# A masked cross attention that keeps keys, queries and results packed on 256 rows and places them by transfers within SBUF

## The chip, the cores and the metric

The kernel runs on one core of one Trainium2 chip. The metric is the device time of one launch in microseconds (us). The program is a decoder of 14 stages that follow one another; the change is in one of them, `L2Cross`, the ninth. PE is TensorE, DVE is VectorE, ACT is ScalarE, POOL is GpSimd, and SP is the queue from which the transfers are issued.

## The reference, cut to what matters

`x` holds 16 batch elements of 112 tokens by 256 features, `ctx` 16 elements of 375 tokens by 256. The stage adds a cross attention of 16 heads of 16 dimensions to `x`, with a mask over the 375 context tokens and with layer norms of queries, keys and values behind their projections:

```python
query = _layernorm(q @ Wq + bq, qn_scale, qn_bias)      # q = _layernorm(x)
key   = _layernorm(kv @ Wk + bk, kn_scale, kn_bias)     # kv = ctx
value = _layernorm(kv @ Wv + bv, vn_scale, vn_bias)
# reshaped to 16 heads of 16
scores = jnp.einsum('bhqd,bhkd->bhqk', query, key) / jnp.sqrt(D_K)
scores = jnp.where(m == 0, NEG_INF, scores)
probs = jax.nn.softmax(scores, axis=-1)
out = jnp.einsum('bhqk,bhkd->bhqd', probs, value)
return out.transpose(0, 2, 1, 3).reshape(bs, -1, D_MODEL) @ Wo + bo
```

## The kernel before

One batch element `n` is worked on in four steps (`NQ = 4`), each with four heads (`HQ = 4`), so that the stage has 64 steps `i = 4n + r`. The text calls the steps by `r`: **quarter 0, 1, 2 and 3** of PE's loop. Each engine runs an order that is written out by hand and waits on semaphores; nothing is reordered.

Each head sits on 32 rows of the 128: one row that carries the softmax shift (or, in the results, the denominator), 16 rows of data and 15 rows of zeros (`Z = 32`). So 256 features take 512 rows (`W = 512`), in four blocks of 128.

One pass of PE's loop, from `scores(i + 1)` to `lowest_turned(i + 1)`:
- `scores(i+1)` (four matmuls, one a head), then `scores_turned(i)` (12 matmuls, the scores once more with the context tokens on the rows), which needs `shifted(i)` from DVE;
- then, each released by one of the four minima that DVE takes from `scores(i+1)` (`lowest`, line 3330, "max" 0 to 3, since the matmuls write the PSUM banks that it has read): two pieces of other work (a and b), then `attend(i-1)` (12 matmuls), and, after the fourth minimum, `lowest_turned(i+1)`, which turns the row minima.

DVE in the same pass takes the four minima, some other work, `shifted(i+1)` as soon as `lowest_turned(i+1)` is there, and then more work that stands in its queue ahead of the next minima. ACT takes `exps(i)`, some other work and `results(i-1)`; POOL zeroes the masked probabilities (`only_kept(i)`, two halves), which `attend(i)` waits for.

The other work by quarter, before: 0: the turn of `x` for n+2 and the spread of the reciprocals of n-2; 1: keys and values of n+2, two of three parts (`keys_values`), the queries of n+1 turned, and the denominators of n-1 gathered by matmuls; 2: the keys of n+1 turned in four blocks (12 transposes), and the output projection of n-2 over four blocks; 3: the third part of keys and values, and the query projection of n+2. The bias of keys and values is added by POOL (`biased`) to a copy that ACT takes out of PSUM. SP loads `ctxT` and the two masks; the weights of the next stage are fetched from the start (`prefetch`).

`L3Cross`, a later stage of the same program with 64 steps of the same kind but without a mask and without norms, already has the packed layout with transfers within SBUF; its rows are in the trace of before.

## Time and profile before

| | |
|---|---|
| median of 3 runs | 3768.4 us (3765.77 to 3771.09) |
| profiled execution | 3750.74 us, its span 3748.9 us |
| PE / PEld / DVE / ACT / POOL busy | 85% / 58% / 49% / 32% / 24% of the span |
| the changed stage | from 2014.4 to 2444.3 us of the span |
| `L3Cross` | from 3239 to 3587.7 us |

The page gives busy time over the whole program; the changed stage is about a ninth of it, so that the stage has to be read alone. In the timeline views each row has a start, the time until the last merged instruction ended, the engine, the line, and after the shapes the count; in brackets stands the idle time before it and what ended it. The difference of two starts is what a group takes in its queue.

### The profile page before, as it was taken

All of it is one profiled execution on the core that took longest, in us unless ns stands there. A gap on an engine that the chain in (4) does not pass through costs nothing. (4 is left out here: it accounts for less than half of the span.)

```text
span 3748.9 us, 76885 instructions
## 1 busy us (share of the span) xinstructions
PE 3184.8 (85%) x30862; PEld 2176.7 (58%) x30862; DVE 1819.2 (49%) x4553; ACT 1188.1 (32%) x2326; POOL 913.9 (24%) x751
## 2 busy tenths in 40 slices
PE   7886999999996875879857899879997788999988
PEld 2333445544566773555624555569996675566655
DVE  7886443344124342442267666643334582355543
ACT  1222222222213322131232655522221452244432
POOL 1000432233000000230624877712111220104000
PEclk9887999999997986998978999979998888999989
DMA  4212000000116011341731111058886210021100
GB/s 147 68 56 75 21 9 8 16 8 0 49 31 43 4 23 30 82 129 45 228 87 33 32 29 28 10 213 331 329 326 234 95 55 15 28 73 54 43 8 15
DMA packets 183358, 291.65 MB, mean 78 GB/s; under 512 B 85585, under 2 KB 153639, under 8 KB 173716
## 3 DMA queue, kind: packets, MB, share of 16 engines
q1 hardware_dynamic: 175572, 266.95, 23.3%
q0 software_dynamic: 7488, 20.46, 1.7%
q8 instruction: 220, 3.60, 0.4%
q14 instruction: 78, 0.64, 0.1%
HBM read 243.33 MB, written 28.48 MB: 73 GB/s over the span
## 5 line engine op out<-in xcount | busy, mean ns | idle before, releaser
L2581 PE MATMUL ps<-L_ffn_xsT,arena 128*128 128x128 f32 x2584 | 305.9, 277 | 0.8 <-DVE L_ffn_xsT L2397 0.7
L2581 PEld LDWEIGHTS ps<-L_ffn_xsT,arena 128*128 128x128 f32 x2584 | 298.5, 194 | 2.9 <-DVE L_ffn_xsT L2397 2.7
L161 POOL TENSOR_TENSOR rstd<-nsc,mhalf 112x4 f32<-112x4 f32 (+1 forms) x24 | 40.1, 1669 | 954.6 <-DVE nsc L154 953.6
L793 POOL TENSOR_TENSOR L_xattn_rn<-L_xattn_ss,mhalf 125x16 f32<-125x16 f32 (+1 forms) x64 | 185.7, 2901 | 324.4 <-DVE L_xattn_ss L847 324.4
L3242 POOL TENSOR_TENSOR L_xattn_pT<-L_xattn_pT,L_xattn_keep 125x678 int32<-125x678 int32 x128 | 190.4, 1509 | 71.9 <-ACT L_xattn_pT L3497 71.9
L686 PE MATMUL ps<-L_attn_prod,arena 128*32 128x448 f32 (+31 forms) x672 | 157.2, 537 | 44.5 <-DVE L_attn_prod L508 44.5
L2489 ACT ACTIVATE L_ffn_silu<-ps,arena 128x128 f32<-128x128 f32 x280 | 102.9, 368 | 269.3 <-PE ps L2581 252.5
L2406 DVE SCALAR_TENSOR_TENSOR L_ffn_hT<-ps,arena,L_ffn_silu 128x128 f32<-128x128 f32 x280 | 97.9, 350 | 156.8 <-ACT L_ffn_silu L2489 156.8
L961 PE MATMUL ps<-arena,L_xattn_cT 128*125 128x512 f32 x384 | 170.3, 596 | 4.3 <-DVE L_xattn_unit L840 4.3
L508 DVE TENSOR_TENSOR L_attn_prod<-arena,L_attn_k 128x448 f32<-128x448 f32 (+10 forms) x336 | 160.4, 545 | 2.3 <-PE ps L686 2.3
L976 PE MATMUL ps<-L_xattn_unit,L_xattn_cn 125*128 125x512 f32 x336 | 159.2, 634 | 0.0
L2594 PE MATMUL ps<-arena,L_ffn_hT 128*128 128x256 f32 x646 | 154.7, 384 | 4.8 <-ACT L_ffn_ys L2498 4.3
L2278 POOL DMA_INDIRECT L_ffn_rows_out<-L_ffn_ys,L_ffn_dest x78 | 80.0, 1025 | 320.0 <-DVE L_ffn_ys L2415 304.2
L845 DVE TENSOR_REDUCE L_xattn_ss<-L_xattn_sq 125x16 f32<-125x1024 f32 (+1 forms) x64 | 78.1, 1220 | 126.3 <-ACT L_xattn_sq L888 126.3
L3929 DVE TENSOR_REDUCE L_xattn_low<-ps 112x1 f32<-112x375 f32 (+1 forms) x192 | 117.8, 667 | 29.0 <-PE ps L4124 29.0
L961 PEld LDWEIGHTS ps<-arena,L_xattn_cT 128*125 128x125 f32 x384 | 69.5, 187 | 104.0 <-issue 77.3
L2594 PEld LDWEIGHTS ps<-arena,L_ffn_hT 128*128 128x128 f32 x646 | 117.4, 191 | 20.8 <-ACT L_ffn_ys L2498 8.0
L3330 DVE CUSTOM_DVE_ANT_0 y<-ps,y 112x375 f32<-112x375 f32 x256 | 124.3, 540 | 6.9 <-PE ps L3603 6.8
L4045 ACT ACTIVATE L_xattn_pT<-ps 125x672 f32<-125x672 f32 x128 | 86.5, 728 | 112.8 <-PE ps L4134 112.8
L2273 POOL DMA_INDIRECT L_ffn_xs<-L_ffn_rows_in,L_ffn_source x78 | 77.5, 993 | 178.9 <-DVE L_ffn_dest L2384 86.2
L1696 PE MATMUL ps<-arena,L_mlp_hT 128*112 128x256 f32 x512 | 117.9, 383 | 0.0
L888 ACT ACTIVATE L_xattn_sq<-ps 125x1024 f32<-125x1024 f32 (+1 forms) x64 | 65.6, 1024 | 163.7 <-PE ps L961 163.7
(574 smaller groups left out, 6713.2 us busy)
## 6 DMA issues: line engine op xcount, KB each, us to landing
arena<-in_L_ffn_up SPq DMA_DIRECT2D x35, 2056.0 KB, 7.7
arena<-in_L_ffn_down SPq DMA_DIRECT2D x35, 1152.0 KB, 8.8
L_xattn_ctxT<-in_ctxT SPq DMA_DIRECT2D x48, 375.0 KB, 3.8
arena<-in_L_ffn_up SPq DMA_DIRECT2D x43, 384.0 KB, 4.5
L_attn_a<-L_attn_skew SPq DMA_DIRECT2D x16, 784.0 KB, 5.8
L_xattn_ctx<-in_ctx SPq DMA_DIRECT2D x30, 375.0 KB
arena<-L_xattn_kp SPq DMA_DIRECT2D x64, 93.8 KB, 3.3
L_xattn_mask<-in_mask SPq DMA_DIRECT2D x32, 164.1 KB, 8.5
```

Source lines behind the costliest of these rows:

```text
L508: nc.vector.tensor_tensor(prod[:, i % RING, :, t0:T], by_batch(q[:, b])[:, :, t0:T], k[:, b, :, PAD + t0 - j:PAD + T - j], ALU.mult).then_ ...
L686: nc.tensor.matmul(by_batch(ps[32 * cg:32 * cg + 32, g % 2, 0:N4])[:, :, t0:T], self.scale[:, w:w + 32], prod[:, i % RING, :, t0:T], start ...
L793: nc.gpsimd.tensor_tensor(rn[0:r, i], ss[0:r, i], core.mhalf[0:r, 0:H], ALU.pow).then_inc(po_r.step("root", i), 1)
L961: ins = nc.tensor.matmul(ps[0:height(i), bank(i) + b, :], lhs, w[:, k, cols], start=(k == 0), stop=(k == KD - 1))
L976: ins = nc.tensor.matmul(ps[:, 4 + 2 * m + b, :], cn[:, t, m * 128:(m + 1) * 128], unit[:, W + t, b * 512:(b + 1) * 512], start=(s == 0), ...
L1696: nc.tensor.matmul(ps[0:T, 4 + u, 0:D], hT[:, i, u * T:(u + 1) * T], self.w2[:, i, :], start=(i == 0), stop=False)
L2489: ins = nc.scalar.activation(silu[:, b % 2], src, ACT.Silu, bias=self.bias(i % WU, m))
L2581: ins = nc.tensor.matmul(ps[:, 2 + b % 4, half * TS:(half + 1) * TS], self.up(i % WU, k, half * HM + m), xsT[:, i % 2, k], start=(k == 0), ...
L2594: ins = nc.tensor.matmul(ps[:, 6 + i % 2, 0:D], hT[:, i % HR, m], self.down(i % WD, m), start=(m == 0), stop=(m == HM - 1))
L3242: nc.gpsimd.tensor_tensor(p, p, keep[:, n % 2].unsqueeze(1).to_broadcast([SP_, 2, ST * TP]), ALU.mult).then_inc(po_e.step("kept", half), 1)
L3330: nc.vector.tensor_tensor_reduce(masked[:, h], ps[0:T, 4 * g + h, 0:S], drop[:, n % 2], -1.0, 3e38, ALU.add, ALU.min, low[:, i % 2, h * Z: ...
L3929: nc.vector.tensor_reduce(heads(low[:, i % 2])[:, h:h + w, 0:1], ps[0:T, b:b + w, 0:S], AX.X, ALU.max, negate=True).then_inc(ve_m.step("ma ...
```

## The change

Queries, keys and results stay packed on 256 rows, in two blocks of 128 (`KD = 2`), with the columns mixed so that the heads of one group of rows lie together. Where the score matmuls need 32 rows a head, SP places the rows by transfers from SBUF to SBUF: four for the keys (`kp` to `kT`), four for the queries (`qk` to `q`), and on the way back one for the denominators (`o` to `den`) and four for the results (`o` to `op`), per batch element.

With it: the keys are turned in two blocks (6 transposes) in quarter 0, the queries in two, the projection has two matmuls; the denominators are 16 rows by 112 that a transfer brings, their reciprocal is taken on 16 rows and spread by two matmuls with `of_head`. DVE adds the bias of keys and values straight from PSUM (`keys_values`), which takes the three copies from ACT and the three additions from POOL. POOL adds the output bias to `x` (`shifted`), once a batch element. The statistics of keys and queries, which DVE took in five pieces over the four quarters, are taken behind `shifted` of quarters 1 and 2, and ACT normalises queries and keys two batch elements ahead, in quarter 3. The turn of `x` moves to quarter 3 and three elements ahead.

```diff
-        self.k = a.take(SP_, ST, self.W)
+        self.k = a.take(SP_, ST, D)
 ...
+            def keys(n):
+                sp.wait_ge(ac_kT.sem, ac_kT.at(n, "kT0"))
+                sp.wait_ge(ve_kT.sem, ve_kT.at(n, "kT1"))
...
+                for h in range(HQ):
+                    sp.dma_start(in_heads(kT[:, n % 2], h), of_rows(kp, h, S)).then_inc(k_in[n % 2], DMA)
...
+            def results(n):
+                sp.wait_ge(ac_p.sem, ac_p.at(NQ * n + NQ - 1, "o"))
...
+                sp.dma_start(den[:, n % 2], o[0:128:Z, n % 2].rearrange("p (j t) -> p j t", j=NQ)).then_inc(o_in[n % 2], DMA)
+                for h in range(HQ):
+                    sp.dma_start(of_rows(op[:, n % 2], h, T), in_heads(o[:, n % 2], h)).then_inc(o_in[n % 2], DMA)
...
+            for n in range(NB):
+                if n + 1 < NB:
+                    keys(n + 1)
+                    queries(n + 1)
+                if n >= 1:
+                    results(n - 1)
+                if n == 1:
+                    run.prefetch(sp)
...
         @block.gpsimd
-            def biased(n, s):
-                nc.gpsimd.tensor_tensor(r, r, self.bkv, ALU.add).then_inc(po_b.step("bias", s), 1)
...
+            nc.gpsimd.memset(q[:, :, :], 0.0).then_inc(zeroed, 1)
+            rows_of(0).then_inc(zeroed, 1)
             nc.gpsimd.memset(low[:, :, :], 0.0).then_inc(zeroed, 1)
+            rows_of(1).then_inc(zeroed, 1)
...
+                if r == 3 and n + 2 < NB:
+                    root_q(n + 2)
+                    root_k(n + 2)
                 only_kept(i)
...
         @block.vector
+            def keys_values(n, s, bank):
+                dve.wait_ge(pe_k.sem, pe_k.at(n, "kv", s))
+                nc.vector.tensor_tensor(raw[:, slot(n, s)], ps[0:SP_, bank, :], self.bkv, ALU.add).then_inc(ve_kv.step("kv", s), 1)
...
+                if r == 0 and n + 1 < NB:
+                    queries(n + 1, 4 * g)
+                    kept(n + 1)
+                if r == 1 and n + 2 < NB:
+                    key_statistics(n + 2, 0)
+                    key_statistics(n + 2, 1)
+                if r == 2:
+                    if n + 2 < NB:
+                        query_variance(n + 2)
+                        key_statistics(n + 2, 2)
+                        for s in range(ST):
+                            key_variances(n + 2, s)
                     if n >= 1:
-                        inverses(n - 1, 4 * g + 3, T)
+                        inverses(n - 1)
+                if r == 3:
+                    if n >= 1:
+                        divided(n - 1, 4 * g + 1)
...
         @block.scalar
+                if r == 3 and n + 2 < NB:
+                    query_normed(n + 2)
+                    keys_normed(n + 2)
...
         @block.tensor
+                if r == 0 and n + 1 < NB:
+                    keys_turned(n + 1, 0, a)
+                    ten.wait_ge(ve_m.sem, ve_m.at(i + 1, "max", 1))
+                    keys_turned(n + 1, 1, b)
...
-                if r == 1 and n >= 1:
-                        denominators(n - 1, 4 * g + 3, T)
```

DVE, from the end of quarter 2 of a batch element in the middle of the stage to the first minimum of quarter 3 (`qm` is written by `shifted`, `st_k` and `st_q` are the statistics of keys and queries, the ISA row on `low` is a minimum). Before:

```order
L3361 TENSOR_TENSOR x<-x,ps 112x256
L3343 TENSOR_TENSOR L_xattn_qm<-L_xattn_q,ps 128x112
L204 BN_STATS stats<-x 112x6
L3307 BN_STATS L_xattn_st_k<-L_xattn_raw 125x6 x2
L3330 ISA y,L_xattn_low<-ps,y 112x375
```

and now:

```order
L3433 TENSOR_TENSOR x<-x,ps 112x256
L3415 TENSOR_TENSOR L_xattn_qm<-L_xattn_q,ps 128x112
L3347 BN_STATS L_xattn_st_q<-y 112x6
L3351 BN_AGGR L_xattn_mv_q<-L_xattn_st_q 112x2
L3353 TENSOR_SCALAR L_xattn_eps_q<-L_xattn_mv_q 112x1
L3378 BN_STATS L_xattn_st_k<-L_xattn_raw 125x6 x2
L3385 BN_AGGR L_xattn_mv_k<-L_xattn_st_k 125x2 x6
L3388 TENSOR_SCALAR L_xattn_eps_k<-L_xattn_mv_k 125x6
L3421 RECIPROCAL L_xattn_inverse<-L_xattn_den 16x112
L3402 ISA y,L_xattn_low<-ps,y 112x375
```

Between `shifted` and the first minimum stood three instructions; now there are thirteen.

ACT, from the end of quarter 3 into quarter 0 (`pT` is written by `exps`, `xT` by the turn of `x`, `y` here holds the queries, the `arena` rows from `raw` are keys or values being normalised). Before:

```order
L3486 COPY L_xattn_raw<-ps 125x512
L3505 COPY L_xattn_least<-ps 128x1
L3507 ACTIVATE L_xattn_o<-ps,L_xattn_least 128x112
L3474 ACTIVATE arena<-L_xattn_raw,L_xattn_off_k,L_xattn_rs_k 125x16x16 x3
L3497 ACTIVATE L_xattn_pT<-ps 125x6x112 x2
```

and now:

```order
L3554 COPY L_xattn_xT<-ps 128x224
L3575 COPY L_xattn_least<-ps 128x1
L3577 ACTIVATE L_xattn_o<-ps,L_xattn_least 128x112
L3530 ACTIVATE y<-y,L_xattn_off_q,L_xattn_rs_q 112x256
L3537 ACTIVATE arena<-L_xattn_raw,L_xattn_off_k,L_xattn_rs_k 125x256 x3
L3567 ACTIVATE L_xattn_pT<-ps 125x6x112 x2
L3560 ACTIVATE L_xattn_kp<-ps,arena 128x375
```

The three normalisations in front of `exps` were those of the values; now they are those of the keys that PE turns in this same quarter 0, with the queries' ahead of them and the packed keys' way out of PSUM (`kp`) behind.

PE, quarter 2. Before:

```order
L3603 MATMUL ps<-arena,L_xattn_q 112x375 x4
L3613 MATMUL ps<-L_xattn_qm,arena 125x112 x12
L3590 MATMUL ps<-ident,arena 128x125 x6
L3627 MATMUL ps<-L_xattn_pT,arena 32x113 x12
L3590 MATMUL ps<-ident,arena 128x125 x6
L3646 MATMUL ps<-arena,L_xattn_on 112x256 x4
L3618 MATMUL ps<-ident,L_xattn_low 128x112
```

and now:

```order
L3648 MATMUL ps<-arena,L_xattn_q 112x375 x4
L3658 MATMUL ps<-L_xattn_qm,arena 125x112 x12
L3630 MATMUL ps<-arena,L_xattn_ctxT 125x512 x2
L3619 MATMUL ps<-arena,L_xattn_xT 112x256 x2
L3672 MATMUL ps<-L_xattn_pT,arena 32x113 x12
L3685 MATMUL ps<-arena,L_xattn_on 112x256 x2
L3663 MATMUL ps<-ident,L_xattn_low 128x112
```

The transposes of the keys have gone to quarter 0, the third part of keys and values and the query projection have come from quarter 3, and the projection (`on`) follows `attend` directly.

## Rows read from the trace of the kernel before

**Rows 1.** Windows: length, busy PE, PEld, DVE, ACT, POOL, PE's clock, DMA share, GB/s

```profile
2086.67:2389.82 303.15, 278.61 (x3384) 173.16 (x3384) 197.53 (x764) 179.27 (x372) 237.70 (x217) 0.98 0.10 28
2389.82:2435.20 45.38, 34.90 (x573) 23.79 (x572) 29.29 (x115) 24.13 (x51) 32.22 (x27) 1.00 0.01 2
2435.20:2444.28 9.08, 5.99 (x52) 4.56 (x52) 2.44 (x7) 1.13 (x3) 0.96 (x1) 1.00 0.00 0
```

**Rows 2.** Timeline of PE, one batch element, quarters 2, 3, 0, 1

```profile
2332.70 0.90 PE L3603 MATMUL ps<-arena,L_xattn_q 32*112 32x375 f32 x8
2335.32 0.86 PE L3590 MATMUL ps<-ident,arena 125*128 125x125 f32 x6
...
2339.86 0.90 PE L3603 MATMUL ps<-arena,L_xattn_q 32*112 32x375 f32 x8
...
2342.02 1.98 PE L3584 MATMUL ps<-arena,L_xattn_ctxT 128*125 128x512 f32 x4 [0.48 <-DVE L_xattn_low L3330]
2343.84 1.03 PE L3571 MATMUL ps<-arena,L_xattn_xT 128*112 128x256 f32 x4
2344.79 0.79 PE L3627 MATMUL ps<-L_xattn_pT,arena 125*32 125x113 f32 x24
...
2345.76 0.90 PE L3603 MATMUL ps<-arena,L_xattn_q 32*112 32x375 f32 x8
...
2348.33 0.60 PE L3640 MATMUL ps<-ident,y 112*128 112x112 f32 x4
...
2349.83 0.90 PE L3603 MATMUL ps<-arena,L_xattn_q 32*112 32x375 f32 x8
...
2356.30 0.60 PE L3577 MATMUL ps<-ident,y 112*128 112x112 f32 x4
...
2357.68 0.90 PE L3603 MATMUL ps<-arena,L_xattn_q 32*112 32x375 f32 x8
```

**Rows 3.** Timeline of DVE in the same batch element

```profile
2340.77 0.73 DVE L3307 BATCH_NORM_STATS2 L_xattn_st_k<-L_xattn_raw 125x6 f32<-125x256 f32 x2
2341.43 0.53 DVE L3330 CUSTOM_DVE_ANT_0 y<-ps,y 112x375 f32<-112x375 f32 x1
...
2346.51 0.43 DVE L3291 BATCH_NORM_STATS2 L_xattn_st_q<-y 112x6 f32<-112x256 f32 x1
...
2347.26 0.54 DVE L3330 CUSTOM_DVE_ANT_0 y<-ps,y 112x375 f32<-112x375 f32 x1
```

**Rows 4.** Timeline of DVE near the stage's start, variances of keys

```profile
2030.89 0.48 DVE L3314 BATCH_NORM_AGGREGATE L_xattn_mv_k<-L_xattn_st_k 125x2 f32<-125x6 f32 x6
...
2050.06 1.43 DVE L3317 TENSOR_SCALAR L_xattn_eps_k<-L_xattn_mv_k 125x6 f32<-125x6 f32 x1
```

**Rows 5.** Timeline of ACT, quarter 3 into 0

```profile
2345.65 0.16 ACT L3505 COPY L_xattn_least<-ps 128x1 f32<-128x1 f32 x1 [0.97 <-PE ps L3627]
...
2346.10 1.59 ACT L3474 ACTIVATE arena<-L_xattn_raw,L_xattn_off_k,L_xattn_rs_k 125x256 f32<-125x256 f32 x3
2347.58 1.33 ACT L3497 ACTIVATE L_xattn_pT<-ps 125x672 f32<-125x672 f32 x2
```

**Rows 6.** Groups by line and shape over the stage's loop

```profile
L3490 ACT ACTIVATE arena<-ps,arena 128x375 f32<-128x375 f32 x30 | 20.0, 667 | 3.2 <-PE ps L3590 3.0
```

**Rows 7.** The later stage `L3Cross`: DVE, SP and PE timelines

```profile
3475.00 0.83 DVE L3940 RECIPROCAL L_xattn_inverse<-L_xattn_den 16x112 f32<-16x112 f32 x1
...
3249.11 2.52 SPq L3837 DMA_DIRECT2D arena<-L_xattn_kp  x4
...
3255.76 0.90 PE L4124 MATMUL ps<-arena,L_xattn_q 32*112 32x375 f32 x8 [1.57 <-DMA L_xattn_q<-L_xattn_qp]
```

**Rows 8.** PE at the stage's start and in its last steps

```profile
2041.18 0.90 PE L3603 MATMUL ps<-arena,L_xattn_q 32*112 32x375 f32 x8
...
2427.64 1.98 PE L3646 MATMUL ps<-arena,L_xattn_on 128*112 128x256 f32 x8 [0.65 <-ACT L_xattn_o L3507]
```

**Rows 9.** Window in one quarter 2 with a lower clock, columns as in rows 1

```profile
2182.00:2184.00 2.00, 2.00 (x21) 1.48 (x21) 1.17 (x5) 1.58 (x3) 0.85 (x1) 0.50 0.00 0
```

More of the change, by code:

```diff
@@ L3190, in _, with context @@
         def _(sp):
-            for n in range(NB):
-                if n == 2:
-                    run.prefetch(sp)
+            def context(n):
                 if n >= 2:
@@ new lines, in queries @@
+            def queries(n):
+                sp.wait_ge(ve_qT.sem, ve_qT.at(n, "q"))
+                if n >= 2:
+                    sp.wait_ge(ve_s.sem, ve_s.at(NQ * (n - 2) + NQ - 1, "shifted"))
+                for h in range(HQ):
+                    sp.dma_start(in_heads(q[:, n % 2], h), of_rows(qk[:, n % 2], h, T)).then_inc(q_in[n % 2], DMA)
+            def results(n):
+                sp.wait_ge(ac_p.sem, ac_p.at(NQ * n + NQ - 1, "o"))
+                if n >= 2:
+                    sp.wait_ge(ve_d.sem, ve_d.at(n - 2, "divided"))
+                sp.dma_start(den[:, n % 2], o[0:128:Z, n % 2].rearrange("p (j t) -> p j t", j=NQ)).then_inc(o_in[n % 2], DMA)
+                for h in range(HQ):
+                    sp.dma_start(of_rows(op[:, n % 2], h, T), in_heads(o[:, n % 2], h)).then_inc(o_in[n % 2], DMA)
@@ new lines, in _ @@
+            for n in range(2):
+                context(n)
+                masks(n)
+            keys(0)
+            queries(0)
+            context(2)
+            for n in range(NB):
[6 more added lines that the diff above has]
+                    run.prefetch(sp)
+                if n + 3 < NB:
+                    context(n + 3)
+                if n + 2 < NB:
+                    masks(n + 2)
@@ L3374, in _ @@
             query_statistics(0, 2)
[L3375 to L3378 removed]
             for s in range(ST):
+                keys_values(0, s, 3 + s)
                 key_statistics(0, s)
@@ L3422, in _ @@
+                if r == 1 and n + 2 < NB:
+                    key_statistics(n + 2, 0)
+                    key_statistics(n + 2, 1)
+                if r == 2:
+                    if n + 2 < NB:
+                        query_variance(n + 2)
+                        key_statistics(n + 2, 2)
+                        for s in range(ST):
+                            key_variances(n + 2, s)
                     if n >= 1:
-                        inverses(n - 1, 4 * g + 3, T)
-                    if n + 1 < NB:
-                        queries(n + 1, 4 * g)
@@ L3517, in _ @@
             act.wait_ge(run.arrived, run.loads)
-            for s in range(ST):
-                keys_values(0, s, 3 + s)
             query_normed(0)
-            keys_values(1, 0, 3)
-            keys_values(1, 1, 4)
+            turned(2, 0)
             keys_normed(0)
-            keys_turned(0, 1, 2)
-            keys_turned(0, 3, 5)
+            keys_turned(0, 1)
+            query_normed(1)
             values_normed(0)
-            keys_values(1, 2, 3)
+            keys_normed(1)
             for i in range(STEPS):
@@ L3575, in queries_turned @@
                 ten.wait_ge(ac_qn.sem, ac_qn.at(n, "qn"))
-                for j in range(NQ):
-                    ins = nc.tensor.transpose(ps[:, bank, j * T:(j + 1) * T], qn[:, j * 128:(j + 1) * 128], core.ident[0:T, 0:T])
-                ins.then_inc(pe_q.step("qT"), 1)
+                transposes(core, ps[:, bank], qn, T, KD).then_inc(pe_q.step("qT"), 1)
             def keys_values(n, s, bank):
@@ L3644, in project @@
                 ten.wait_ge(ve_d.sem, ve_d.at(n, "divided"))
-                for j in range(NQ):
-                    ins = nc.tensor.matmul(ps[0:T, bank, 0:D], on[:, n % 2, j * T:(j + 1) * T], self.wo[:, j, :], start=(j == 0), stop=(j == NQ - 1))
+                for m in range(KD):
+                    ins = nc.tensor.matmul(ps[0:T, bank, 0:D], on[:, n % 2, m * T:(m + 1) * T], self.wo[:, m, :], start=(m == 0), stop=(m == KD - 1))
                 ins.then_inc(pe_o.step("out"), 1)
@@ L3723, in _ @@
                     queries(n + 2, b)
-                if i + 1 == STEPS:
-                    spread(n - 1, b)
+                if r == 3:
+                    if n + 3 < NB:
+                        turn(n + 3, a)
+                    if n >= 1:
+                        if i + 1 < STEPS:
+                            ten.wait_ge(ve_m.sem, ve_m.at(i + 1, "max", 1))
+                        spread(n - 1, b)
                 if i >= 1:
@@ L3749, in _ @@
             project(NB - 2, 4)
-            denominators(NB - 1, 1, 0)
             spread(NB - 1, 2)
```

360 lines of the change are left out of this document (153 added, 207 removed).

## The prediction

> **What bounds the kernel now.** The page first: the changed stage is 430 us of 3749, and the other 13 stages keep their instructions, so everything below is about that stage. Next the windows: in the middle of the stage PE is busy 278.6 of 303.2 us, POOL 237.7, DVE 197.5, ACT 179.3 [rows 1]. That looks like a PE bound, but the reader is to see in PE's timeline where it waits: one batch element takes 24.98 us from 2332.70 to 2357.68, in quarters of 7.16 (quarter 2), 5.90 (3), 4.07 (0) and 7.85 (1) [rows 2]. In each quarter PE stands still only where the other queues hold it: in quarter 3 the keys and values start 0.48 late, on the first minimum of DVE [rows 2]. PE goes on 0.59 after DVE starts its first minimum (2341.43 to 2342.02) [rows 2, 3]. So what counts is not DVE's busy share but how much work stands in its queue between `shifted` and the next minima; there is little slack, and whoever puts work there pays. The same holds for ACT between its `results` and `exps`.
>
> **The change, quarter by quarter.** I lay the new queues out with the in-queue times of before (start to next start) and count from the start of `scores`.
>
> PE's own work falls. Two blocks of keys instead of four save 6 transposes, 0.86. Two projection matmuls of four save half of 1.8, so 0.9. The denominators and half of the turned queries go: 2356.30 to the next `scores` at 2357.68 is 1.38, of which `lowest_turned` (0.2) and two transposes (0.22) stay, so about 0.95 [rows 2]. Together 2.7 us a batch element. If PE alone counted, 14 elements would give 38 us. I do not expect to see it, for these reasons:
>
> Quarter 2. PE now has `keys_values` and the query projection here, as in the old quarter 3, and DVE has two pairs of statistics ahead of its minima (0.66 each [rows 3]) instead of the update of `x`, its statistics and one pair; its first minimum starts at about 1.6, as in the old quarter 3. So `attend` starts at 5.0 (before: 2339.86 to 2344.79 = 4.93) [rows 2]. The projection waits for `results` of the `attend` just ahead of it, which the second half of the key transposes used to cover; uncovered it is 0.79 of `attend` and 0.65 of idle time, as in the last steps [rows 8]. Then 0.9 for two projection matmuls and 0.2: 5.0 + 1.44 + 0.9 + 0.2 = 7.55, against 7.16.
>
> Quarter 3. Behind `shifted` (ended 0.57 into the quarter: the pair at 2340.77 was at 0.91, with 0.34 of statistics of `x` ahead of it that have moved away, an estimate by the query's similar 0.43) stand now: variance of the queries 0.75, a pair of statistics 0.66 [rows 3], six aggregations 0.48 [rows 4] and the epsilon 0.1 (an estimate by one of these six), the reciprocal on 16 rows 0.8 (0.83 busy in the later stage [rows 7]; the one before, of 112 rows by 16, stood elsewhere). Sum 3.35: DVE's first minimum starts there, not at 1.57. PE goes on at 3.95; its second piece waits for the second minimum, 1.07 behind the first's start (2347.26 to 2348.33 [rows 2, 3]): 4.4, the spread of four short matmul passes 0.6, `attend` and `lowest_turned` 0.97 (2344.79 to 2345.76 [rows 2]): 6.0, against 5.90. PE has only 3.8 of work there, so 2.2 us of PE's gain is idle time.
>
> Quarter 0. ACT: `attend` of quarter 3 starts at 5.0; `results` starts 0.86 later and the next in the queue another 0.45 later (2344.79, 2345.65, 2346.10 [rows 2, 5]), so at 6.35. Then the queries' normalisation 0.5 and the keys' three 1.48 (2346.10 to 2347.58, the same shapes for the values [rows 5]): 8.3, which is 2.3 into quarter 0. PE wants to turn these very keys at 1.7 and starts at 2.45; 0.8 for both blocks and 0.75 for `attend`: 4.0. The turned queries reuse the bank of the first block, so they wait for ACT: `exps` 2.3 to 3.55, then the packed keys, 0.67 [rows 6]: 4.25. With 0.22 and 0.25: 4.75, against 4.07.
>
> Quarter 1. Nothing new ahead; the denominators and half of the turned queries fall away: 7.85 - 0.95 = 6.9, and with `divided` on 224 instead of 448 columns and now in quarter 0, about 6.7. The bias additions on DVE (not in the trace in this shape; between the 0.42 of the query's 256 columns and, by columns, 0.8) lie behind the minima, beside 3.6 us of PE's matmuls for keys and values, and are hidden: uncovered they would cost 0.7 in quarter 1.
>
> Sum 7.55 + 6.0 + 4.75 + 6.7 = 25.0 against 24.98: nothing, for the twelve elements in the middle.
>
> Transfers. In the later stage, four transfers of keys and four of queries took from 3249.11 to 3255.76, 6.65 us, until the scores started [rows 7]. Here the packed keys are ready at 4.3 of quarter 0 and the scores want them at the start of quarter 3, 16 us later; SP has 13 issues of 0.63 (2.52 for four [rows 7]) and three loads, some 10 us of 25. The next stage's weights are now issued in the second element, behind `results`, 5 us of SP; still hidden. Results have two quarters. What hides all this is the loop; at both ends there is no loop.
>
> The ends. Start: POOL writes 2.1 us more (`q`, twice `kT`, less `k` and `qn`), the keys and values of element 1 (5.5) now come before the first key transposes, and 6.65 of transfers stand before the first scores; against it, the weights' scaling leaves the path. From the last of element 0's work I get the first scores at 45 instead of 41.18 [rows 8], +4 (3 to 5). Tail: 9.08 [rows 1] from the last `attend` on; the gathering matmuls, the widening on ACT and the wide projection (-2.5) give way to five transfers, 5 * 0.63 + 1.6 of landing (6.65 - 8 * 0.63) = 4.8: +2.3 (1 to 3).
> The first two elements have no projection or no reciprocals: there quarter 1 gives its 1.2 twice and quarter 3 0.6: -3. In the last two there are no statistics, keys or values, PE's saving is real: 45.38 [rows 1] shrinks by 1.3 + 2.0 (a quarter 1 without denominators, a quarter 2 without transposes and half the projection) and 0.8 + 0.9, less 1: -4.
>
> Total: 0 + 4 + 2.3 - 3 - 4 = -0.7 us. Against the profiled execution: 3750.7 - 0.7 = 3750.0. The runs' median is 17.7 above that execution, so 3768.4 - 0.7 = 3767.7; I say 3768.
>
> **Rules of the skill that speak against it.** A small DVE operation can be held up by POOL: the epsilon of the keys took 1.43 us once, while six small ones take 0.48 [rows 4]. In quarter 3 the two epsilons now stand in the chain that PE waits for; by my layout POOL has nothing to do just then. The Trainium skill, "SBUF — State Buffer", section "SBUF: two separate sides", says that POOL and a DVE operation in a two-port mode hold a shared pair of ports exclusively, and the other blocks for the whole instruction. The trace agrees where both met; by that rule the forecast stands only while POOL is idle there, otherwise the rival below holds.
>
> **The rivals.**
> 1. PE's saving comes through. That needs the minima to start early in quarter 3 and the keys to be normalised in time. For it: quarter 3's 3.35 is a sum of seven in-queue times, and waits of PE can shift into one another. Half of the lost 2.7, over 12 elements, is 16 us: 3752; all of it 3736. Against: ACT's order is fixed. Chance 0.22 for anything faster than 0.2%.
> 2. The clock. PE now stands still for 2.2 us in quarter 3 and for 0.8 in quarter 0. In a quarter 2 of before PE's clock fell to half (0.50 at 2182 to 2184 [rows 9]), behind short matmuls; three such drops in the middle explain 303.15 against 12 times 24.98 = 299.8, so 1.1 each [rows 1, 2]. Place: quarter 3; one drop in each element, less the three: + 9 * 1.1 = 10 us, 3778. It decides from seven more drops on (7.5 us). Against: in the stretch from 2389.82, where PE was busy for 34.9 of 45.4 us, the clock was 1.00 [rows 1]. Chance 0.17. The Trainium skill, "TensorE: Matmul & The Clock Gate", section "HAM oscillation — how this bites in real kernels", says that waits between bursts throw the array back to its lower clock; by it this would be the likelier way.
> 3. DVE's chain is longer than laid out: an epsilon held by POOL for up to 1.3 (1.43 less 0.1 [rows 4]) in quarter 3, once or twice an element, + 12 * 1.3 = 16 us: 3784. It needs POOL to be late from quarter 2. Chance 0.11.
> 4. The forecast, within 0.2%: 0.50.
>
> **The numbers.** A change of 0.2%, 7.5 us, is about what a measurement of this kernel can tell from none. Quarters that I may have wrong by 0.3 us, over 12 elements, make 4 us; the two ends 2 more. Own range 3761 to 3776. For 8 in 10 it reaches to half of rival 1 and to rivals 2 and 3: 3755 to 3784. Faster 0.22, same 0.50, slower 0.28.
>
> **What would show it.** In the profile after: PE's timeline with quarters of 7.5, 6.0, 4.8 and 6.7; a wait of about 2 us before the turn of `x` or the spread, ended by DVE's minimum; the key transposes waiting for ACT's normalised keys and the turned queries for `kp`; the projection waiting for `o`; no wait of `scores` for a transfer but at the start; first scores 4 us later. The forecast is wrong if quarter 3 is near 4.5 (DVE's queue was not the bound), if the clock is 0.50 in many windows, or if `scores` waits for transfers in the loop.

## The result, and the profile after

The changed kernel is slower: 3790.53 us median (3782.62 to 3795.19, 6 runs) against 3769.32 us (3765.77 to 3773.78) for the kernel before, run beside it. The ratio is 1.0052, 95% interval 1.004 to 1.0065. The prediction said 3768 us, range 3755 to 3784, "same" the likeliest. It was wrong, and the time lies outside the range.

The changed stage takes 448.7 us in place of 428.5, 20.2 more, about the whole of the difference of 21.2 between the medians. (The two profiled executions are further apart, 3793.1 and 3748.9 us; the other 24 us lie outside the stage, where the instructions are the same, and in the changed kernel run again they are 4. So the stage is read from the profiles and the whole from the medians.) Cut at the first `scores`, at the quarter 3 of element 1, at the quarter 3 of element 13, and at the last `scores`:

| part of the stage, us | before | after | difference | forecast |
|---|---|---|---|---|
| start, until the first `scores` | 26.7 | 32.0 | +5.3 | +4 |
| first two elements | 45.5 | 44.0 | -1.5 | -3 |
| twelve elements in the middle | 303.2 | 314.4 | +11.3 | 0 |
| last steps, until the last `scores` | 33.8 | 35.0 | +1.2 | -4 |
| tail | 19.3 | 23.3 | +4.0 | +2.3 |

The forecast cut the last two parts at the last `attend` and not at the last `scores`. By its own cut they are 45.4 and 47.2 us (+1.8, forecast -4), and 7.7 and 11.1 us until TensorE is done (+3.4, forecast +2.3).

The windows of the changed kernel, columns as in [rows 1]: the middle, the last steps (here they reach into the last one), and the tail.

```profile
2106.95:2421.39 314.44, 267.39 (x3145) 164.94 (x3145) 211.80 (x766) 145.64 (x314) 201.40 (x192) 0.89 0.19 54
2421.39:2460.37 38.98, 28.09 (x476) 19.45 (x476) 24.50 (x96) 18.70 (x40) 27.74 (x24) 0.87 0.08 21
2460.37:2480.10 19.73, 12.36 (x93) 8.29 (x93) 7.34 (x17) 2.38 (x6) 5.58 (x5) 0.50 0.03 7
```

The seventh value is TensorE's granted clock. In the middle it is 0.89 where it was 0.98 [rows 1]. At the end it is 0.87 and 0.50, where it was 1.00 throughout. That is the first thing to see, and most of the document follows from it.

TensorE's timeline for one element, quarters 2, 3, 0 and 1, the counterpart of [rows 2] (L3648 is `scores`):

```profile
2308.65 0.90 PE L3648 MATMUL ps<-arena,L_xattn_q 32*112 32x375 f32 x8
...
2310.85 1.98 PE L3630 MATMUL ps<-arena,L_xattn_ctxT 128*125 128x512 f32 x4 [0.66 <-DVE L_xattn_low L3402]
...
2313.62 0.79 PE L3672 MATMUL ps<-L_xattn_pT,arena 125*32 125x113 f32 x24
2315.08 1.12 PE L3685 MATMUL ps<-arena,L_xattn_on 128*112 128x256 f32 x4 [0.66 <-ACT L_xattn_o L3577]
...
2316.22 0.90 PE L3648 MATMUL ps<-arena,L_xattn_q 32*112 32x375 f32 x8
2316.98 0.92 PE L3658 MATMUL ps<-L_xattn_qm,arena 32*125 32x112 f32 x24
2320.07 0.41 PE L210 MATMUL ps<-ident,L_xattn_xn 112*128 112x112 f32 x2 [2.16 <-DVE L_xattn_low L3402]
2320.53 1.14 PE L3679 MATMUL ps<-L_xattn_inverse,arena 16*128 16x112 f32 x4
2321.60 1.36 PE L3672 MATMUL ps<-L_xattn_pT,arena 125*32 125x113 f32 x24
...
2323.27 1.61 PE L3648 MATMUL ps<-arena,L_xattn_q 32*112 32x375 f32 x8
2324.66 1.46 PE L3658 MATMUL ps<-L_xattn_qm,arena 32*125 32x112 f32 x24
2326.05 1.51 PE L3636 MATMUL ps<-ident,arena 125*128 125x125 f32 x6
2327.49 0.79 PE L3672 MATMUL ps<-L_xattn_pT,arena 125*32 125x113 f32 x24
...
2328.65 0.90 PE L3648 MATMUL ps<-arena,L_xattn_q 32*112 32x375 f32 x8
```

The reader is to see three things. The waits are where the prediction put them: 0.66 for the projection's `o`, 2.16 for the first minimum of quarter 3. Behind that wait the same instructions take longer: L3672 takes 0.79 us in quarter 2 and 1.36 in quarter 3, the scores 0.90 and then 1.61, the turned scores 0.92 and 1.46. And at 2327.49, in quarter 0, they are back at 0.79. Quarters 2 and 1 take 7.57 and 6.50 us (forecast 7.55 and 6.7); quarters 3 and 0 take 7.05 and 5.38 (forecast 6.0 and 4.75).

VectorE in quarter 3, the counterpart of [rows 3]:

```profile
2316.23 0.42 DVE L3433 TENSOR_TENSOR x<-x,ps 112x256 f32<-112x256 f32 x1 [2.08 <-PE ps L3685]
2316.57 0.26 DVE L3415 TENSOR_TENSOR L_xattn_qm<-L_xattn_q,ps 128x112 f32<-128x112 f32 x1
2316.75 0.42 DVE L3347 BATCH_NORM_STATS2 L_xattn_st_q<-y 112x6 f32<-112x256 f32 x1
...
2317.42 0.15 DVE L3353 TENSOR_SCALAR L_xattn_eps_q<-L_xattn_mv_q 112x1 f32<-112x1 f32 x1
2317.49 0.74 DVE L3378 BATCH_NORM_STATS2 L_xattn_st_k<-L_xattn_raw 125x6 f32<-125x256 f32 x2
2318.15 0.49 DVE L3385 BATCH_NORM_AGGREGATE L_xattn_mv_k<-L_xattn_st_k 125x2 f32<-125x6 f32 x6
2318.68 0.17 DVE L3388 TENSOR_SCALAR L_xattn_eps_k<-L_xattn_mv_k 125x6 f32<-125x6 f32 x1
2318.76 0.84 DVE L3421 RECIPROCAL L_xattn_inverse<-L_xattn_den 16x112 f32<-16x112 f32 x1
2319.53 0.47 DVE L3402 CUSTOM_DVE_ANT_0 y<-ps,y 112x375 f32<-112x375 f32 x1
```

The first minimum starts 3.31 us into the quarter (2316.22 to 2319.53); the forecast was 3.35. The two epsilons take 0.15 and 0.17, so POOL does not hold them up. The first row also shows what the experiments use: ahead of the update of `x`, VectorE waits 2.08 us for the projection.

The clock, in windows of this stretch (quarter 3, quarter 0, and the stretch in which the instructions are slow):

```profile
2316.22:2323.27 7.05, 4.83 (x64) 3.27 (x63) 5.08 (x23) 1.91 (x5) 5.22 (x8) 0.81 0.00 0
2323.27:2328.65 5.38, 5.38 (x67) 3.97 (x66) 3.53 (x12) 4.45 (x10) 2.06 (x3) 0.61 0.01 3
...
2320.50:2327.00 6.50, 6.47 (x66) 4.97 (x67) 3.78 (x15) 3.64 (x9) 3.15 (x4) 0.51 0.01 3
```

From just after the end of the 2.16 us wait until 2327 the clock is at its lower level, 1.2 in place of 2.4 GHz, while TensorE is busy for all of the stretch. The text calls such a stretch a fall. Over the elements 2 to 12 the fall begins between 0.3 us before and 1.6 us after the end of this wait. In quarter 0 TensorE then has no idle time at all (5.38 of 5.38 us), so the slow matmuls are themselves what the quarter takes. Windows of half a microsecond over the whole middle show 12 such falls in 12 elements, 68.3 us at the lower level in all; before there were 3, with 10.2 us. A fall lasted 3.4 us in four elements and 6.8 us in the other eight. Against the 10.57 us that quarters 3 and 0 take together without a fall (below, e10), a fall of 3.4 us cost 0.8 to 0.9 and one of 6.8 us 1.8 to 2.2 us.

### The profile page after: what moved, and what is told of

The parts are those of the page before. It is cut to its first block and busy times, and to the rows that moved or that the text cites. A ratio compares the mean times of both kernels' runs of the same rounds, so it can differ in the third digit from the quotient of the medians.

```text
span 3793.1 us, 76365 instructions
## 1 busy us (share of the span) xinstructions
PE 3173.7 (84%) x30540; PEld 2169.6 (57%) x30540; DVE 1840.0 (49%) x4555; ACT 1142.3 (30%) x2246; POOL 866.8 (23%) x720
## 5 line engine op out<-in xcount | busy, mean ns | idle before, releaser
L2581 PE MATMUL ps<-L_ffn_xsT,arena 128*128 128x128 f32 x2584 | 313.7, 281 | 32.9 <-DVE L_ffn_xsT L2397 23.6
L686 PE MATMUL ps<-L_attn_prod,arena 128*32 128x448 f32 (+31 forms) x672 | 157.0, 537 | 45.4 <-DVE L_attn_prod L508 45.4
```

The lines of the kernel that those rows point to most:

```text
L686: nc.tensor.matmul(by_batch(ps[32 * cg:32 * cg + 32, g % 2, 0:N4])[:, :, t0:T], self.scale[:, w:w + 32], prod[:, i % RING, :, t0:T], start ...
L2581: ins = nc.tensor.matmul(ps[:, 2 + b % 4, half * TS:(half + 1) * TS], self.up(i % WU, k, half * HM + m), xsT[:, i % 2, k], start=(k == 0), ...
```

## The experiments

The theory (A): with the granted clock at 1.00, the new quarters would add up to the old ones as forecast. The VectorE work behind `shifted` in quarter 2 makes TensorE wait 2.16 us in quarter 3, the clock falls behind that wait, and the slow matmuls of quarters 3 and 0 make the loss. The rival (B): the moved VectorE work and the new waits make the loss by themselves, and the lower clock costs nothing. Each kernel ran beside the kernel before. The absolute times named in the expectations of the first four are on the scale of the first comparison, 3769 for the kernel before; in theirs it had 3754.9, so the differences are what to compare. "Middle" is the time of the twelve elements, with the falls of the clock in them and the time at the lower level, counted in windows of half a microsecond.

| kernel | median, minus before beside it, us | ratio, 95% interval | stage | middle | falls, us low |
|---|---|---|---|---|---|
| before | | | 428.5 | 303.2 | 3, 10.2 |
| changed | +21.2 | 1.0052, 1.004 to 1.0065 | 448.7 | 314.4 | 12, 68.3 |
| e10, changed again | +18.5 | 1.0054, 1.0036 to 1.0073 | 443.9 | 311.5 | 11, 58.0 |
| e1, nine fillings | +8.4 | 1.0029, 1.0014 to 1.0043 | 437.4 | 305.1 | 0 |
| e5, four fillings | -1.6 | 0.9997, 0.9984 to 1.001 | 427.9 | 298.5 | 4, 13.7 |
| e4, reciprocal early | -2.4 | 0.9997, 0.9984 to 1.001 | 420.9 | 290.6 | 4, 13.7 |
| e2, statistics early | -27.0 | 0.9937, 0.992 to 0.9955 | 399.9 | 273.0 | 0 |
| e3, both early | -24.8 | 0.9943, 0.9928 to 0.9959 | 406.1 | 276.9 | 0 |
| e6, statistics spread | -37.2 | 0.9895, 0.9873 to 0.9916 | 396.4 | 267.5 | 1, 6.8 |
| e7, ends too | -40.7 | 0.9894, 0.9875 to 0.9914 | 388.4 | 265.7 | 0 |
| e8, before with an idle | +28.5 | 1.0064, 1.0039 to 1.0089 | 458.4 | 328.6 | 7, 23.9 |
| e9, other wait filled | +76.1 | 1.0194, 1.0175 to 1.0213 | 508.4 | 368.8 | 12, 164 |

(The middle of e1 is twelve times its element of 25.43 us. The low time of e9 is twelve falls of 13.7 us. The profile behind stage and middle is of one execution, the median of five or more, and the two can differ by some us: e4 and e6 do by 5.)

**Filling the wait: e1, e5.** TensorE gets extra matmuls among the scores of quarter 3, in a region that the real scores overwrite:

```diff
                 for h in range(HQ):
+                    if h == 3 and i % NQ == 0 and 2 <= n <= NB - 1:
+                        for w in range(9):    # 4 in e5
+                            nc.tensor.matmul(ps[0:T, 4 * g + h, 0:128], self.wo[:, 0, 0:T], self.wo[:, 1, 0:128], start=True, stop=True)
                     p = slice(h * Z, (h + 1) * Z)
```

> The changed kernel, with nine more TensorE matmuls of 128 columns (some 2 us) put among the scores of each quarter 3, in the stretch in which TensorE waited 2.16 us for the first minimum. They write a region that the real scores then overwrite, so the results are the same; TensorE only has more to do. Theory A (the clock: the 2.16 us idle in quarter 3 makes the granted clock fall to 0.50 for 3.4 or 6.8 us in each element, and that costs about 1 us of an element): the clock stays at 1.00 in the middle elements, quarter 3 takes 6.1 to 6.3 in place of 7.1 and quarter 0 4.7 to 4.9 in place of 5.3, 10 to 14 us less in all, 3776 to 3781. Theory B (the clock only falls where VectorE is waited for anyway; the quarters are longer because the moved VectorE work and the new waits are): 3790 or up to 5 us more, quarter 3 stays at 7.1.

Measured: no fall in the middle, and quarter 0 at 4.67 us as expected. Quarter 3 takes 6.67, not 6.2: nine fillings are more than the wait can hold, TensorE is busy 6.50 of 6.67 us there. About 13 us less than the changed kernel (+8.4 in place of +21.2). More work on the busiest engine made the kernel faster, which B doesn't allow; the size was left for e5.

> The changed kernel with four of the nine filling matmuls (some 0.9 us of TensorE work that leaves the results as they are). The nine kept the clock at 1.00, but made quarter 3 take 6.67 us, because they held up the work behind them; four leave the first minimum as the last to come, as in the changed kernel, and VectorE's chain as it is. Theory A (the clock costs 0.87 us in quarter 3 and 0.64 us in quarter 0): TensorE's idle falls to about 1.2 us, the clock stays at 1.00, quarter 3 takes 6.0 and quarter 0 4.67; 1.5 us per middle element, 16 to 20 us less than the changed kernel, that is 0 to +4 us beside the kernel before. Theory B (the clock is only a sign, the 2.16 us of VectorE work cost it all): within 3 us of the changed kernel, +20 beside the kernel before. If the clock still falls with 1.2 us idle, the same as B in time, with the clock at 0.50 as before.

Measured: 0.9997 of the kernel before, 22.8 us less than the changed kernel by the differences of the medians. The windows of one element, quarters 2, 3, 0 and 1, columns as in [rows 1]:

```profile
2204.30:2211.88 7.58, 6.25 (x70) 3.79 (x69) 4.56 (x15) 4.16 (x10) 3.13 (x3) 1.00 0.41 112
2211.88:2217.79 5.91, 5.41 (x73) 3.83 (x72) 5.08 (x23) 1.70 (x4) 4.08 (x7) 1.00 0.00 0
2217.79:2222.45 4.66, 3.68 (x66) 2.53 (x65) 3.49 (x12) 4.59 (x11) 3.11 (x3) 1.00 0.02 5
2222.45:2228.96 6.51, 6.37 (x66) 3.14 (x66) 4.54 (x14) 1.45 (x4) 6.43 (x6) 1.00 0.28 80
```

With the clock at 1.00 the quarters are 7.58, 5.91, 4.66 and 6.51, in sum 24.66; the forecast was 7.55, 6.0, 4.75 and 6.7, in sum 25.0. TensorE's wait before the turn of `x` is 0.44 us, and not the 1.2 that I had expected of four fillings. VectorE's busy time in quarter 3 is the same 5.08 us as in the changed kernel. Quarter 3 takes as long as a quarter 3 of the changed kernel without a fall (5.91, below), so the fillings changed nothing of the schedule but TensorE's idle time. A holds, B is refuted. Four falls are left in the middle all the same, all of 3.4 us, in quarters 3 and 0.

**The changed kernel again: e10.**

> The changed kernel as it is, once more beside the kernel before, for the size of the difference and to see whether the clock falls as often in another execution. If the drops belong to the schedule: 1.004 to 1.0065 of the kernel before (15 to 24 us more), 12 falls in the 12 middle elements, most of them 6.8 us long. If they were a matter of that one execution: fewer than 8 falls.

Measured: 1.0054, 11 falls. Two elements of this execution are worth more than the sum, since there nothing was edited. Quarters 3 and 0 of one element without a fall, and of one with a long fall:

```profile
2190.55:2196.46 5.91, 3.69 (x65) 2.47 (x64) 5.08 (x23) 1.81 (x4) 4.08 (x7) 1.00 0.00 0
2196.46:2201.12 4.66, 3.68 (x66) 2.53 (x65) 3.49 (x12) 4.59 (x11) 3.11 (x4) 1.00 0.01 4
2240.51:2247.51 7.00, 4.78 (x65) 3.22 (x64) 5.08 (x23) 1.91 (x5) 5.17 (x8) 0.82 0.00 0
2247.51:2252.89 5.38, 5.38 (x66) 3.98 (x66) 3.53 (x12) 4.43 (x10) 2.10 (x3) 0.60 0.01 3
```

The same instructions, the same idle before the first minimum: 10.57 us without the fall, 12.38 with it. A long fall costs 1.8 us.

**The other wait: e9.** The fillings stand in quarter 0 (`i % NQ == 1`, three of them) in place of quarter 3.

> The changed kernel with three filling matmuls (0.4 to 0.6 us of TensorE work that leaves the results as they are) in quarter 0, where TensorE waits 0.84 us for the first minimum; the wait of 2.16 us in quarter 3 stays whole. It asks which idle the clock follows. Theory A1 (the one long wait of quarter 3 brings the clock down): the clock falls in nearly every element as in the changed kernel, and the time is within 4 us of it, or up to 5 us more. Theory A2 (any idle of the element counts alike, so filling a short wait helps as much as filling a part of the long one): the clock stays up in most elements, 10 us or more less than the changed kernel, as the four matmuls in quarter 3 gave 20.

Measured: much slower than either theory said. The clock fell in every element, as A1 has it, from 3.7 to 4.0 us into quarter 3, where the long wait ends; filling in quarter 0 did not help, as A2 wanted it. The time was off by 50 us. Quarter 3 and quarter 0:

```profile
2276.18:2283.38 7.20, 5.04 (x65) 3.41 (x64) 5.08 (x23) 1.91 (x5) 5.37 (x8) 0.76 0.01 2
2283.38:2292.69 9.31, 9.31 (x72) 6.56 (x72) 3.54 (x12) 4.68 (x10) 2.80 (x3) 0.50 0.00 0
```

Quarter 0 takes 9.31 in place of 5.38 us, all of it busy and at the lower clock. The fillings stand ahead of the last scores, on which the minima and everything behind them wait, and take some 1.5 us of it at the lower rate; the other 2.4 come from the rest of the quarter, all of which now runs at 0.50 in place of 0.61. Each fall lasts 13.7 us. 3.9 us in each of 15 elements make 59; the stage is 59.7 us longer than the changed kernel's, and the medians 55 to 58. Three such matmuls here lost over 50 us, where four in quarter 3 gained over 20. Why the clock stayed down for twice as long isn't settled.

**Moving the cause away: e2, e3, e4.** VectorE's own wait of 2.08 us ahead of the update takes the statistics (e2), the reciprocal (e4) or both (e3):

```diff
                 if r == 2:
                     if n + 2 < NB:
                         keys_values(n + 2, 2, 4 * g)
                         queries_biased(n + 2, 4 * g + 1)
+                        query_variance(n + 2)         # e2, e3
+                        key_statistics(n + 2, 2)
+                        for s in range(ST):
+                            key_variances(n + 2, s)
+                    if n >= 1:                        # e3, e4
+                        inverses(n - 1)
                     if n >= 2:
                         update(n - 2, 4 * g + 2)
```

(and they go from behind `shifted`, where they stood.)

> The changed kernel, with the moved statistics of quarter 2 (query_variance, the third key_statistics, the key_variances; 2.0 us of VectorE) put ahead of the update of x and of the shifted queries, into 2.08 us in which VectorE waited for the projection; the reciprocal stays behind. Theory A (the clock and the idle of quarter 3 that brings it down): TensorE's idle in quarter 3 falls from 2.16 to about 0.2, the clock stays up; quarter 3 takes 4.9 to 5.2, quarter 0 4.7 to 4.9, about 2.6 us per element, 14 elements: 36 us less, 3754 (3748 to 3762). Theory B (schedule alone, the clock has no part): 2.0 x 14 = 28 us less, 3762, with quarter 0 still at 5.3. Theory C (the 2 us is needed elsewhere: quarter 3 is bound by ScalarE's or POOL's chain at 6 us as it was before the change): quarter 3 at 5.9 to 6.2, 15 us less, 3775.

> As the run with the statistics ahead of the update, and the reciprocal of the denominators (0.77 us) ahead of it too. VectorE then starts the first minimum of quarter 3 about 1.3 us into the quarter, when the scores have just come. Theory A: no idle before the first minimum beyond the minimum's own 0.5; but 2.8 us of work stand in 2.08 us of waiting, so the update and the shifted queries come 0.7 us later and quarter 2 may grow by that. The sum against the run with the statistics alone: -0.8 in quarter 3 and up to +0.7 in quarter 2, so between 0 and 10 us less: 3744 to 3754. Theory C (quarter 3 held at 6 us by ScalarE or POOL): same as that run within 2 us, or 10 us more if quarter 2 grows.

> The changed kernel, with only the reciprocal (0.77 us of VectorE) put ahead of the update of x in quarter 2. TensorE's idle in quarter 3 becomes 1.4 us in place of 2.16. Theory A: if an idle of 1.4 us still brings the clock down, 0.77 x 14 = 11 us less, 3780; if it doesn't, 11 + 12 = 23 us less, 3768. Theory B (no part of the clock): 11 us less, 3780, whatever the clock shows.

Measured: e2 is 48 us faster than the changed kernel and 27.0 faster than the kernel before (A said 36 less than the changed one, B 28, C 15, so all three were too small). In e2, quarter 3 of an element: VectorE's first minimum, and TensorE's next work.

```profile
2293.78 0.83 DVE L3421 RECIPROCAL L_xattn_inverse<-L_xattn_den 16x112 f32<-16x112 f32 x1
2294.55 0.47 DVE L3402 CUSTOM_DVE_ANT_0 y<-ps,y 112x375 f32<-112x375 f32 x1
```

```profile
2293.25 0.90 PE L3647 MATMUL ps<-arena,L_xattn_q 32*112 32x375 f32 x8
2294.01 0.92 PE L3657 MATMUL ps<-L_xattn_qm,arena 32*125 32x112 f32 x24
2295.08 0.41 PE L210 MATMUL ps<-ident,L_xattn_xn 112*128 112x112 f32 x2
```

The minimum starts 1.30 us into the quarter and TensorE shows no wait. Quarter 3 takes 3.89 us, quarter 0 4.67, the element 22.65. I had expected 4.9 at best for quarter 3, and C 6: neither ScalarE nor POOL was the next bound there. Of the saving of TensorE's work that the first rival of the prediction spoke of, 2.7 us an element, most is there (24.98 - 22.65 = 2.33), and it needed only this.

What is left in quarter 0 is a wait of 0.84 us before the turn of the keys:

```profile
2299.69 0.83 PE L3635 MATMUL ps<-ident,arena 125*128 125x125 f32 x6 [0.84 <-DVE L_xattn_low L3402]
```

```profile
2297.97 1.57 ACT L3536 ACTIVATE arena<-L_xattn_raw,L_xattn_off_k,L_xattn_rs_k 125x256 f32<-125x256 f32 x3
```

The row names VectorE's minimum, but TensorE here also waits for ScalarE's normalised keys, and these are ready at 2299.54, 0.15 us before it goes on. That is the wait for ScalarE that the prediction had in quarter 0 (the expectation of e9 took it for one on the minimum).

e3 is no better: its quarter 3 takes 4.21. The 2.8 us of work do not fit into the wait, the shifted queries come later, and the turned scores wait for them; I had put that delay into quarter 2, and it shows in quarter 3. The row of e3, and the wait for the first minimum that is left in e4:

```profile
2274.94 0.92 PE L3656 MATMUL ps<-L_xattn_qm,arena 32*125 32x112 f32 x24 [0.52 <-DVE L_xattn_qm L3415]
```

```profile
2259.13 0.41 PE L210 MATMUL ps<-ident,L_xattn_xn 112*128 112x112 f32 x2 [1.51 <-DVE L_xattn_low L3402]
```

e4 decides between A's two branches: with this wait of 1.51 us, only 4 falls are left in the middle, most elements have quarter 3 at 5.25 and quarter 0 at 4.67, and the time is 23.6 us less than the changed kernel. 23 was the number of "the clock stays up"; 11 that of the schedule alone. It does not show that the length of the single wait decides: e5, with no wait over 0.84 us in most elements, has four falls too.

**The idle without the change: e8.**

```diff
                     if n + 2 < NB:
                         key_statistics(n + 2, 0)
+                        for w in range(5):
+                            nc.vector.bn_stats(junk[:, 30 * (n % 7) + 6 * w:30 * (n % 7) + 6 * w + 6], self.bkv[:, 0:D])
```

> The kernel before, with five more bn_stats (1.75 us of VectorE, into a tile that nothing reads) ahead of the first minimum of quarter 3, so that TensorE's idle there is 2.2 us in place of 0.48; nothing else of the change is in it. Theory A (an idle of some 2 us in quarter 3 brings the clock down in this loop, whatever the layout): the clock is at 0.50 for 3.4 us or more in nearly each element as in the changed kernel; 1.75 us and 1 to 1.5 us for the clock, 14 elements: 38 to 46 us more than the kernel before. Theory B (the drops come from something else in the new layout, short matmuls or transfers): the clock stays, 1.75 x 14 = 24 us more.

Measured: +28.5 us, between the two theories. TensorE's wait in quarter 3 is 2.12 us, as meant. Two quarters 3, one with a fall and one without:

```profile
2279.29:2288.45 9.16, 7.04 (x67) 3.75 (x66) 5.80 (x20) 2.05 (x4) 3.98 (x3) 0.81 0.08 11
2307.52:2315.06 7.54, 5.42 (x67) 3.12 (x66) 5.80 (x20) 2.05 (x4) 3.98 (x3) 1.00 0.09 26
```

A fall costs 1.4 to 1.7 us here, but there are 7 in the middle, not 12, and each of 3.4 us. Six of them come behind the wait in quarter 3, where the kernel before had none; the seventh is in quarter 2, as its three were. So the old layout, given the same wait, shows falls in quarter 3 in half of the elements, and the new one in nearly all. The wait is a cause and not the only condition; in the new layout a wait for ScalarE's `kp` and less matmul work stand around it (TensorE busy 267.4 of 314.4 us in the middle, against 278.6 of 303.2 [rows 1]). Which of these makes the rest was not tried.

**Further on the same way: e6, e7.** e6 is e2 with `key_statistics(n + 2, 0)` between the two `keys_values` of quarter 1, and with `statistics(n - 2)` ahead of `shifted` in quarter 3. e7 is e6 with the first queries' transfers on ScalarE's queue and a semaphore of their own for the denominators.

```diff
-            queries(0)                                    # SP, at the start
+            for h in range(HQ):                           # ScalarE, ahead of values_normed(0)
+                act.dma_start(q[h * Z + 1:h * Z + 1 + HD, 0].rearrange("p (j s) -> p j s", j=NQ), qk[h % 2 * 64:(h % 2 + 1) * 64, 0, h // 2 * T:(h // 2 + 1) * T]).then_inc(q_in[0], DMA)
...
-                dve.wait_ge(o_in[n % 2], (n // 2 + 1) * (HQ + 1) * DMA)
+                dve.wait_ge(d_in[n % 2], (n // 2 + 1) * DMA)
```

> The kernel with the statistics ahead of the update (23 to 27 us faster than the kernel before), and two more moves of VectorE work into its own waits: key_statistics(n+2, 0) between the two keys_values of quarter 1 (it waits 1.03 us there), and statistics(n-2) of quarter 3 ahead of the shifted queries (it waits 0.82 us there). If the first minimum is what ends TensorE's waits of 0.66 us in quarter 2 and 0.84 us in quarter 0: 0.65 less in one and 0.35 less in the other, 1.0 us per element, 14 us less, 3714 on the scale on which the kernel before has 3755. If ScalarE or POOL is right behind (POOL's masks end 1.3 us before the weights times values in quarter 2, ScalarE's 2 x exp in quarter 0 follow keys_normed at once): only one of the two comes through, 5 to 9 us less.

> As the run with the statistics spread, and two changes of the transfers at the ends: the four transfers of the first queries are issued by ScalarE's queue beside SP's four for the first keys, and the denominators have a semaphore of their own, so that their reciprocal doesn't wait for the four transfers of the results. Start: the first scores waited for the last transfer of queries, whose issue came after the keys'; 2.0 to 2.5 us less. Tail: the last reciprocal and the spread (2.1 us) run beside the transfers of the results, about 2 us less. Together 4 us less (3 to 5) than that run. Rival: a transfer's fixed time and not its turn in the queue sets both; then 0 to 2 us less.

Measured: e6 has quarter 2 at 6.95 (0.63 less) and quarter 0 unchanged at 4.67, so one of its two moves came through, and the middle is 5.5 us shorter than in e2. In quarter 0 the first minimum then waits for the scores themselves and starts no earlier, 0.97 us into the quarter; and TensorE's wait of 0.84 us ends there 0.14 us behind ScalarE's normalised keys, as in e2. e7's median is 3.5 us below e6's, but the two ratios, 0.9894 and 0.9895, can't be told apart. Its profile has the tail at 20.0 us in place of 21.8; about 2 were expected of the reciprocal. The start gained next to nothing against the changed kernel (e6's own profile had a wait of 8.79 us there, where the other profiles of this layout on one queue have 7.8 to 7.9). TensorE's windows until the first scores, of e7 and then of the changed kernel:

```profile
2040.95:2048.63 7.68, 0.17 (x3) 0.04 (x1) 5.12 (x20) 3.03 (x6) 1.78 (x3) 0.66 0.68 113
```

```profile
2055.15:2063.01 7.86, 0.00 (x1) 0.03 (x1) 4.95 (x19) 3.88 (x8) 2.16 (x3) 0.67 0.26 73
```

The stretch is as long with two queues, while the busy share of the DMA engines (last value but one) went from 0.26 to 0.68 and the bytes per second only from 73 to 113. SP's four issues of keys in e7:

```profile
2042.25 2.59 SPq L3222 DMA_DIRECT2D arena<-L_xattn_kp  x4
```

They were out at 2044.84, and the scores waited for the keys until 2048.63, so that the queries' turn behind them was not what set the start. One thing stands against a comparison of the two windows: in e7 SP issues the load of the next `ctxT`, 375 KB, right behind the keys (2044.89), 3.7 us ahead of the scores, and in the changed kernel only 1.5 us ahead of them (2061.47). Part of the higher share is this load, and it may have held up the keys; that was not tried.

e7 beats both kernels: 40.7 us, 1.06% below the kernel before.

## Why the prediction was wrong, by its own steps

- **The quarters.** Right. With the clock up they are 7.58, 5.91, 4.66 and 6.51 (e5) against 7.55, 6.0, 4.75 and 6.7. All waits that it named are there: 2.16 us for the minimum, 0.66 for `o`, the key transposes behind ScalarE (they start 2.54 us into quarter 0 in e5, forecast 2.45), none of `scores` for a transfer in the loop.
- **The sum.** Without the many falls it nearly comes out, in part by luck. The stage of e5 is 427.9 us against 428.5: -0.6, where the prediction had -0.7. By the prediction's own cuts the start is +3.5 (forecast +4), the first two elements -0.5 (-3), the middle -4.7 (0), the last steps -2.4 (-4) and the tail +3.4 (+2.3). The middle gained what the two ends lacked: quarter 1 is 6.51 and not 6.7, the sum of the quarters 24.66 and not 25.0.
- **Rival 2, the clock: the step that failed.** The sum put the lower clock in the middle at nothing; the rival had its mechanism and its place right, but got a chance of 0.17 and did not enter the forecast. It was also mis-sized: "one drop in each element, less the three: + 9 * 1.1 = 10 us". Measured are 12 falls in 12 elements, 8 of them twice as long as those of before. The three of before cost 1.3 each and not 1.1 (their quarters 2 take 8.44, 8.44 and 8.41 us, the others 7.15; the prediction's 303.15 - 299.8 left out that the first of the twelve elements is 0.5 shorter). The twelve of after cost 18.8 together: four of 0.8 to 0.9 and eight of 1.8 to 2.2. Less the 3.8 of before, the clock takes some 15 us more in the middle, and the schedule gives 3.6 of them back, which leaves the 11.3 measured. The same by e5: 314.4 - 298.5 = 15.9 us above it in the middle, where it still has 4 falls; outside the middle 4.9 us more. All of the loss over e5's stage is 448.7 - 427.9 = 20.8 us.
- **The argument against it.** "In the stretch from 2389.82, where PE was busy for 34.9 of 45.4 us, the clock was 1.00." A busy share averages over the waits. Up to the last `attend` no single wait in that stretch was longer than this one of the kernel before:

```profile
2402.89 0.79 PE L3627 MATMUL ps<-L_xattn_pT,arena 125*32 125x113 f32 x24 [1.11 <-DVE L_xattn_low L3330]
```

  I compared a share of 77% spread over waits of 1.1 us and less with one wait of 2.16 us, and these are different cases: the changed kernel's middle is busy for 85% and has the falls. The runs with a shorter wait in quarter 3 have fewer: 12 and 11 falls with 2.16 us, 4 with 1.51 (e4), 4 with 0.44 (e5), none with 0.52 (e3) and none with no wait left (e1, e2). The length of the wait alone does not give the number, as e4 beside e5 and e8 beside the changed kernel show.
- **The rule of the skill.** The Trainium skill, "TensorE: Matmul & The Clock Gate", section "HAM oscillation — how this bites in real kernels", says that waits between bursts of matmuls throw the array back to its lower clock and that this is paid at every tile. The trace agrees in direction: 12 of 12 elements. The waits of the page's example are longer than this one of 2.16 us, so that the page alone did not say that it would happen here; the prediction took it as saying so, and then chose the other way on its own argument.
- **Rival 3, POOL.** It did not come: the epsilons took 0.15 and 0.17 us. POOL was not wholly idle there, it worked on the queries' scale between the two (2317.67 to 2318.72) and overlapped the second by 0.04 us.
- **Rival 1, the saving comes through.** Not in the changed kernel; in e2, by a change of order alone.
- **The start** was 5.3 us later in the changed kernel's profile and 3.6 in e10's (30.3 against 26.7), so the term of +4 stands.
- **The tail.** +3.4 us by the prediction's cut, in e5 and e2 as in the changed kernel, and its clock is 0.50 there in all three, where it was 1.00 before. The forecast of +2.3 had no term for it, and what the lower clock costs there was not measured.

## What to carry to other kernels

When a change takes work from the busiest engine and leaves an idle time in its place, price that idle time twice: for its length, and for a lower clock behind it. A busy share averaged over another stretch is no argument against the second price: 77% kept the clock at 1.00 here and 85% did not. A run in which the wait is filled settles it. Before giving up such a saving, look for an engine that waits elsewhere in the same round: 2.0 us of VectorE work put into VectorE's own wait turned 21 us lost into 27 us gained. And matmuls that do nothing useful can be a test of the clock, but where they stand decides: four in the long wait gained 23 us, three in the next quarter, ahead of scores that others wait for, lost 55.

## What was not expected of the hardware

- A fall of the clock lasted 3.4, 6.8 or 13.7 us in these traces, while TensorE was busy through nearly all of it, and cost 0.6 to 0.9 us (3.4 us long) or 1.8 to 2.2 us (6.8 us long) of an element of the changed kernel. In the old layout one of 3.4 us cost 1.3 in quarter 2 and 1.4 to 1.7 in quarter 3.
- With a wait of 2.12 us the kernel before showed falls behind it in 6 of 12 elements (e8), the changed one with 2.16 us in 12 and in 11. What the clock follows besides the single wait stays open.
- Eight transfers within SBUF on two queues took as long until the scores as on one (7.68 and 7.86 us), with the DMA engines' busy share at 0.68 in place of 0.26; a load of 375 KB is part of that share.
